# A two-block gated transformer kernel on one core: one clip pass in five moved to another engine, first key transfers shared, the entry of the second attention reordered

## The reference, cut to what matters

```python
# block 1: cross attention, 16 heads of 16, with projections, softmax replaced by
s = where(scores >= 0, scores + 1, 1 / (1 - scores)); attn = s / sum(s)
# block 2: mixture of 64 experts, top 8, capacity 128, and a shared expert of 512
# block 3: attention of layernorm(x) on the raw context, plain softmax
out = softmax(q k^T) v
# block 4: 256 -> 1024, butterfly of 10 stages, gelu, butterfly, 1024 -> 256
```

## Time and profile before

| | |
|---|---|
| median of 3 runs | 1233.26 us (1229.75 to 1236.8) |
| the profiled execution | 1231.84 us |
| its span in the profile | 1229.6 us |
| PE busy | 1034.0 us, 84% |
| VectorE (DVE) busy | 817.2 us, 66% |
| ScalarE (ACT) busy | 702.2 us, 57% |
| GpSimd (POOL) busy | 360.6 us, 29% |
| mean granted TensorE clock | 0.927 of full speed |

### The profile page before, as it was taken

How to read it: one execution, slowest core, us unless ns; L and a number is a source line. 1 busy time by engine, 2 the same in 40 slices (tenths; PEclk the granted TensorE clock), 3 DMA queues, 4 the chain that set the end, 5 groups by cost and what they waited for, 6 DMA issues and landing times.

```text
span 1229.6 us, 17473 instructions
## 1 busy us (share of the span) xinstructions
PE 1034.0 (84%) x5635; PEld 751.7 (61%) x5635; DVE 817.2 (66%) x2051; ACT 702.2 (57%) x1351; POOL 360.6 (29%) x313
## 2 busy tenths in 40 slices
PE   4688888888876688998899976888898989899888
PEld 2354544544444577887687755657676767767567
DVE  4468778777778766755667658687567577664543
ACT  1899878988975433565554421364455455544542
POOL 2000000000000003778777631124334251423223
PEclk9779988988887888999999996899999999999998
DMA  6564435434121323788988644331312133120000
GB/s 145 122 153 137 129 95 167 120 82 129 52 73 69 128 61 104 184 203 199 245 198 184 146 119 92 88 109 26 106 46 80 37 104 82 50 56 1 20 18 18
DMA packets 97401, 128.41 MB, mean 104 GB/s; under 512 B 26976, under 2 KB 69344, under 8 KB 97056
## 3 DMA queue, kind: packets, MB, share of 16 engines
q1 hardware_dynamic: 82448, 105.73, 30.0%
q0 software_dynamic: 12288, 18.88, 8.5%
q10 hardware_dynamic: 2576, 2.69, 1.0%
HBM read 66.15 MB, written 30.70 MB: 79 GB/s over the span
## 4 chain that ended last, share of the span: by engine, by line
PE 51%; DVE 26%; ACT 9%; issue 6%; POOL 3%; DMA 2%; SPq 2%; ACTq 2%; DVEq 0%; POOLq 0%
PE psum L912 6%; PE psum L1098 6%; PE psum L1083 5%; PE psum L1001 4%; PE psum L928 4%; PE psum L819 3%; DVE stats L1363 3%; PE psum L795 3%; PE psum L865 3%; PE psum L1030 2%; DVE weights L1484 2%; DVE peaks L1764 2%; PE psum L960 2%; PE psum L741 2%; DVE normed L1404 2%
## 5 line engine op out<-in xcount | busy, mean ns | idle before, releaser
L1863 POOL TENSOR_SCALAR vareps<-moments 128x4 f32<-128x4 f32 x32 | 10.4, 326 | 529.2 <-DVE moments L1366 529.2
L795 PE MATMUL psum<-q_stack,k_stack 96*128 96x512 f32 (+1 forms) x256 | 123.2, 511 | 39.2 <-DVE weights L1484 24.8
L1297 ACT ACTIVATE weights<-psum 128x512 f32<-128x512 f32 x160 | 94.1, 597 | 71.7 <-PE psum L795 60.7
L1484 DVE SCALAR_TENSOR_TENSOR weights<-psum,weights 128x512 f32<-128x512 f32 x160 | 102.5, 681 | 43.2 <-ACT weights L1162 43.0
L1883 POOL DMA_INDIRECT expert_sums<-made,sum_rows x64 | 105.4, 1647 | 59.3 <-DVE made L1734 38.6
L1910 POOL TENSOR_TENSOR hidden<-hidden_whole,hidden 128x512 fp32r<-128x512 f32 x64 | 82.3, 1287 | 114.2 <-DVE hidden L1812 114.2
L1030 PE MATMUL psum<-k_stack,q_stack 96*128 96x256 f32 x256 | 88.2, 395 | 31.9 <-DVE peaks L1764 20.0
L1764 DVE TENSOR_REDUCE peaks<-psum 128x2 f32<-128x308 f32 x256 | 107.0, 469 | 12.1 <-PE psum L1032 11.6
L912 PE MATMUL psum<-feat_parts,w_shared_up 128*128 128x512 f32 x384 | 100.5, 412 | 10.7 <-DVE shared_silu L1608 6.3
L1098 PE MATMUL psum<-w_con_high,hidden 128*128 128x256 f32 x512 | 102.2, 298 | 0.1
L1812 DVE CAST hidden<-hidden_whole 128x512 fp32r<-128x512 f32 x64 | 52.7, 823 | 71.6 <-ACT hidden_whole L1326 70.3
(11 more groups left out here) (211 smaller groups left out, 2390.9 us busy)
## 6 DMA issues: line engine op xcount, KB each, us to landing
expert_w<-in_expert_w SPq DMA_DIRECT2D x64, 384.0 KB
q_stack<-q_stage SPq DMA_DIRECT2D x96, 128.0 KB, 3.0
q_stack<-q_stage SPq DMA_DIRECT2D x174, 64.0 KB, 2.0
expert_sums<-zeros SPq DMA_DIRECT2D x6, 1408.0 KB, 8.2
fetched<-expert_sums SPq DMA_DIRECT2D x16, 512.0 KB, 4.8
rows_scratch<-rows SPq DMA_DIRECT2D x8, 640.0 KB, 3.4
k_raw<-in_k SPq DMA_DIRECT2D x16, 300.0 KB
x<-in_x SPq DMA_DIRECT2D x8, 512.0 KB, 4.8
```

Source lines behind the costliest of these rows:

```text
L795: T.matmul(to, k[0:row, head_at(head), :], q[0:row, head // 2, :], start=True, stop=True).then_inc(scored, 1)
L1297: A.activation(weights1[n % 6][:, :], score_bank[n % 2], ACT.Exp).then_inc(exped, 1)
L1484: V.scalar_tensor_tensor(weights[n % 9][:, :], score_bank[n % 5], 1.0, weights[n % 9][:, :], ALU.add, ALU.max).then_inc(weighted, 1)
```

## The change

It does these things:

- First attention: the clip of each group's fifth chunk (32 of 160) is done by VectorE (`clip_last`) and listed one round earlier, behind the weights of the group's first pair; the log of that chunk waits for it on a semaphore of its own. An empty step is put between `turn_att` and `att_feats`.
- Start: of batch 0's 12 key DMAs ScalarE issues 6 (places 0 and 1); SP issues its queries of places 0 and 1, then queries and keys of places 2 and 3. GpSimd's clearing waits for the first norm. Two load semaphores are merged.
- Into the second attention: SP issues the loads of half 0's sums (in four DMAs, by pairs of tiles) and of the first two quarters of keys ahead of the barrier, once all sums have been written. VectorE adds by pairs of tiles and takes the statistics of each pair behind it. GpSimd's adds for half 1 wait for the four key residuals instead of the norm of half 0.
- Half 1: statistics and norm stand behind the maxima of half 0, the turned queries behind them, and all four sends are SP's. `PEAKS_SECOND` places the 16 maxima of half 1 at c = 1 to 11.

```diff
@@ after_steps
-    return [turn[0:2], divide[0:2] + turn[2:4], divide[2:4], [("turn_att", h)], [("att_feats", h)],
+    return [turn[0:2], divide[0:2] + turn[2:4], divide[2:4], [("turn_att", h)], [], [("att_feats", h)],
@@ plan_first
             plan += [("weight", n) for n in sets[i - 1]]
+        if i + 1 < len(sets) and len(sets[i + 1]) == 1:
+            plan.append(("clip_last", sets[i + 1][0]))
...
-        plan += [("clip", n) for n in now]
+        if len(now) > 1:
+            plan += [("clip", n) for n in now]
@@
-PEAKS_SECOND = (-1, -1, -1, -1, 1, 2, 3, 4, 5, 6, 7, 7, 8, 8, 9, 9)
+PEAKS_SECOND = (1, 2, 2, 3, 4, 4, 5, 6, 6, 7, 8, 8, 9, 10, 10, 11)
@@ plan_last
-    plan = [("fetch", 0), ("load_k1", 0, 0), ("load_k1", 0, 1)]
+    plan = []
...
-    beside_peaks = {4: norm_units("q1", 1)[:2], 7: norm_units("q1", 1)[2:],
-                    9: [("turn_q1", 1), ("send_q1", 1, 0), ("send_q1_a", 1, 1)]}
     for n in range(HT * PAIRS // 2):
         plan.append(("peak", 0, n % HT, n // HT))
-        plan += beside_peaks.pop(n, [])
         if n in LATE_AT:
             late.step()
-    plan.append(("peaks", 0))
-    plan += [("send_q1", 1, two) for two in range(2, PAIRS // 2)]
+    plan += [("peaks", 0)] + norm_units("q1", 1)
     late.step()
-    plan += peak_units(1, -1)
+    plan += [("turn_q1", 1)] + [("send_q1", 1, two) for two in range(PAIRS // 2)]
+    late.step()
     plan.append(("scores1", 0))
@@ ScalarE
                 if b == 0:
                     A.wait_ge(keys_split, 1)
-                    to_key_stack(A, 0)
+                    to_key_stack(A, 0, (0, 1))
...
             def log(n):
-                A.wait_ge(clipped, n + 1)
+                if n % 5 == 4:
+                    A.wait_ge(clipped_last, n // 5 + 1)
+                else:
+                    A.wait_ge(clipped, n // 5 * 4 + n % 5 + 1)
@@ VectorE
+            def clip_last(n):
+                if n >= 9:
+                    V.wait_ge(weighed, weighed_by(n - 9))
+                V.wait_ge(scored, n + 1)
+                V.tensor_scalar(weights[n % 9][:, :], score_bank[n % 5], -1.0, 0.0, ALU.mult,
+                                ALU.max).then_inc(clipped_last, 1)
...
-            def add_experts(h, i):
+            def add_experts(h, a):
                 if h == 0:
-                    V.wait_ge(fetched_in[i], 16)
-                    if i:
-                        V.wait_ge(x_first, i)
-                    V.tensor_tensor(half_of(0), half_of(0), fetched[i][:, :, :], ALU.add).then_inc(x_first, 1)
+                    tiles = slice(2 * a, 2 * a + 2)
+                    for i in range(SUMS):
+                        V.wait_ge(first_sums[SUMS * a + i], 32)
+                        if i:
+                            V.wait_ge(x_first, SUMS * a + i)
+                        V.tensor_tensor(x[:, tiles, :], x[:, tiles, :], fetched[i][:, tiles, :],
+                                        ALU.add).then_inc(x_first, 1)
+                    V.wait_ge(x_first, SUMS * (a + 1))
+                    for t in range(2 * a, 2 * a + 2):
+                        tile_stats(norm_no["q1", 0], 0, t)
@@ GpSimd
                     elif h == 1:
-                        G.wait_ge(ln_normed, HT * (norm_no["q1", 0] + 1))
+                        G.wait_ge(keys_split, BATCH + 4)
...
             def clear_rest():
+                G.wait_ge(ln_normed, HT)
@@ SyncE
-                send(S, q_stage, q_stack[h % 2][:, :, :], q_in[h % 2])
+                together = (0, 1) if h == 0 else range(4)
+                send(S, q_stage, q_stack[h % 2][:, :, :], q_in[h % 2], places=together)
+                if h == 0:
+                    S.wait_ge(keys_split, 1)
+                    for r in (2, 3):
+                        send(S, q_stage, q_stack[0][:, :, :], q_in[0], places=(r,))
+                        to_key_stack(S, 0, (r,))
...
+            def fetch_first():
+                for i in range(SUMS):
+                    S.wait_ge(scattered[i], 16 * (EXPERTS // SUMS))
+                for a in range(2):
+                    for i in range(SUMS):
+                        S.dma_start(fetched[i][:, 2 * a:2 * a + 2, :], sum_dram[i][2 * P * a:2 * P * (a + 1), :].rearrange(
+                            "(t p) f -> p t f", p=P)).then_inc(first_sums[SUMS * a + i], 16)
...
                     S.drain().then_inc(stage_over, 1)
+                    if n == 2:
+                        fetch_first()
+                        load_k1(0, 0)
+                        load_k1(0, 1)
                     S.wait_ge(stage_over, 5 * n)
```

37 lines of the change are left out of this document (20 added, 17 removed).

## The result

The changed kernel takes 1261.19 us in the median of 4 runs (1259.42 to 1264.49), the kernel before 1233.36 beside it (4 runs): a ratio of 1.0237, with a 95% interval of 1.0204 to 1.0269. It is 28 us slower; the prediction said 26 us faster. The profiled execution took 1262.6 us, its span is 1260.5.

What follows compares the result with a forecast made beforehand. ScalarE was taken to bound the first attention, a chain across engines the passage into the second. Start −7, steady −15, tail +1 and passage −5 sum to −26: from the median of 1233.26 to 1207.3 us, range 1192 to 1228.

Steps and rivals of the forecast that it cites:

- ScalarE is the bound there: First attention's body, 35 to 355 us: ScalarE, at work 289.66 of 320 us, sets the pace.
- relief term: First attention, steady: 32 clips of 0.62 us leave ScalarE, 19.8 us less at most, taken as −20.
- Rival 3: First attention: no new waits, half of the old one goes; steady −27, in all −38, 1195 us; 12%.
- rival 1: First attention: VectorE's lag decides everywhere, steady part gives 0, start and passage stay; −11, 1222 us; 20%.
- Rival 4: First attention: VectorE becomes the bound, keeps its waits, its clips add 21.8 us; in all +11, 1244 us; 9%.
- steady part: First attention's loop: −20 clips, −6 empty step, +11 new waits, so −15 us; bounds −35 and +21.8.
- (a) to (d): Passage: early sums and moved GpSimd adds −2.9 us, half 1's norm work leaving half 0's maxima −5.4, its return net 0.
- (d): Passage: half 1's norm and turned queries return behind half 0's maxima, about 11 us instead of 8 before first scores; net 0.
- (b): Passage: GpSimd's adds for half 1 no longer slow a shared expert's residual (2.768 us, usually 0.692); some 0.6 us won.
- (e): Second attention's loop: four of half 1's maxima, hidden in a wait before, join it; 3.4 us.
- (f): Passage: SP sends half 1's 24 query pieces before fetching half 2's sums; up to 4 us of VectorE's wait.
- Rival 2: Passage gives nothing, since its loop stalls for half 2's sums; in all −21, 1212 us; 16%.

Runs made afterwards that it cites:

- b3: a3 without the fifth chunks' clip (log reads scores with scale 0, output differs), so ScalarE has 32 passes less, VectorE none more: 1230.95 us, ratio 0.9986.
- b2: a3 with 32 VectorE passes over constants in the place of its clips, for which nobody waits: 1241.22 us, ratio 1.0098.
- a1: The changed kernel without the empty step, fifth chunks' clips still on VectorE: 1248.44 us, ratio 1.0115.
- d3: b4 with an empty step behind the norm, so all behind the norm comes one step later: 1242.36 us, ratio 1.0087.
- c4: b4 with only the 16 maxima of half 1 at the changed kernel's places in the loop: 1232.36 us, ratio 0.9988.
- a3: The changed kernel without the empty step and with all 160 clips on ScalarE: 1231.40 us, ratio 0.9976.
- a4: The changed kernel with half 2's sums and two key quarters issued ahead of half 1's last two pairs of query sends: 1261.96 us, ratio 1.0227.
- b4: a3 with half 1's norm, turned queries, sends and maxima placed as in the kernel before: 1222.73 us, ratio 0.9925.
- d2: b4 with the additions to x alone one step later: 1220.32 us, ratio 0.9914.
- d4: b4 with the norm's statistics one step earlier, in one step with the additions: 1222.57 us, ratio 0.9917.
- d1: b4 with the norm's statistics alone one step later, directly ahead of the norm: 1237.29 us, ratio 1.0044.
- e1: d1 with four PE products, results overwritten, ahead of PE's wait for the normed rows: 1230.65 us, ratio 0.9968.

## Why the prediction was wrong

**The step that failed first is "ScalarE is the bound there".** It was read from busy shares, 289.66 of 320 us. b3 is the test: 32 passes gone and nothing added is worth 4.1 us in the traced execution and nothing in the medians, not 19.8. The relief term of −20 was at least about five times too large. My reading, which no run tests by itself: per group of heads every engine waits for another in turn (scores, exponentials, weights, bank), and a pass off one link returns only where that link ends a wait. Rival 3 fell with it. ScalarE's idle time was also not "mostly one wait": the 15.0 us are half of its 30.3.

**VectorE's load** was sized about rightly, by the pass (0.684 against 0.68) and by the price: I took +11 for the new waits, and b2 measures 11.2 for the 32 passes alone (15.0 by the ratios), with 1 to 2 more for the log's wait. But I had set it against 20. The clips then come out at +8.6 by themselves (17.1) where −9 stood; rival 1 (VectorE's lag takes the relief) named the mechanism and stopped at 0. Rival 4 had the sign and half of the mechanism: VectorE's clips do go on the path, but at 11.2 us and not at their full 21.8, and it is not the bound (busy 253.13 of 320 us in a1, 237.03 in the changed kernel). Rival 4's bound for the steady part, +21.8, was passed too, since neither it nor the forecast gave the empty step a loss.

**The empty step** is the term with the largest error. I had counted it as −6 (bounds 0 and −15), for the wait for the attention rows, and never asked what it does to the fifteen steps behind it. That wait did go, and as large a one stands before the gate's rows. The step as put costs 18.8 alone and 22.8 on top of the clips (392.7 to 415.5). d3 shows that moving all behind the norm is enough for that (23.3 us). What the traces show there is gate and shift in one round, with VectorE waiting 17.1 us for the gate product (1.2 before); which of the units behind the norm costs the time (gate, shift, exponential, top, counts) was not tried apart. In sum the steady part is +29.6 in the loop (323.7 to 353.3) where −15 stood.

**Start.** −7 against −7.3: right, both terms within 0.6 us; clip at 28.0 (28.5 forecast), norm 1.39 us, ScalarE's six issues 6.01. The issues began 1.5 us earlier where the norm was to give 1.0. The price of an issue is the trace's: 1.00 us each while SP issues too, 0.64 for SP's 24 later ones. The rule of the Trainium skill (Trainium Kernel Development and Optimization, Key Constraints) is that issuing from several engines saves issue time only. Read as the prediction read it, six issues at a lone queue's price, ScalarE would have been free sooner than at 27.35. It was the keys' landing (first scores at 27.19) and then the scores that set the clip, so its time can't tell the two.

**Tail.** 59.4 to 64.5 us from the last exponential to the next stage over all kernels, 60.4 before and 62.2 after; +1 can't be told from 0.

**Passage.** Up to the first exponential the forecast holds: last write to there 62.7 and 57.6 us, −5.1 where (a) to (d) summed to −8.3; the second add waits no more, the maxima of half 0 take 15.9 instead of 20.1, but (d), "net 0", is +2.3 (9.1 to 11.4). (b) came out as forecast: GpSimd's adds lie behind the first norm's followers, and no residual of the shared expert takes over 0.724 us (2.768 before). The last residual, which the prediction's −3 would have had held by the moved adds, took 0.693 at 770.8; the adds had ended at 769.9, so this run doesn't test it. The failed term is the 3.7 for (e) and (f): halves 0 and 1 of the loop take 105.9 instead of 94.6 us, 11.3 lost. It is (e), the places of the maxima: c4 alone loses 9.6 us of median (7.8 by the ratios), more than the 7.4 that I had called the most for (e) and (f) together; (f) is there (3.10 us of wait, 4 at most forecast), a3 has the same plan without such a wait and a passage no shorter (165.2 us), and a4 removes its cause without a gain in the medians. I priced the four maxima that join the loop and not the other twelve, which all move to later places, up to c = 11. Which of the places does it was not tried. Rival 2 (the passage gives nothing) was nearer, and it too stopped at 0.

By parts, before rounding: −7.3 + 29.6 + 6.2 = +28.5; the medians differ by 27.8, the profiled executions by 30.8.

## What to carry to other kernels

A busy share of 90% doesn't make an engine the bound where each waits for the others in turn: before pricing a relief, take the work away and see what comes back (here a fifth at most). In a hand-written order, an empty step isn't a wait of one step; it moves every step behind it, and for each of these one has to ask whether it now shares a round with the step that feeds it. A profile of one execution prices a stage to a few us only; compare it with the ratios of the medians before splitting a loss into parts. The best kernels found keep the start, the early loads, the pairwise statistics and GpSimd's later adds, and leave half 1 as it was: b4, d2 and d4 (the last two with additions or statistics one step off), at 0.9914 to 0.9925 of the time before.

## What the runs showed of the hardware that was not expected

Passes of VectorE for which nobody waits cost 0.35 us each (b2, 11.2 over 32; 0.47 by the ratios) of the 0.680 us that they last, though VectorE is idle a quarter of the loop. An issue of a small DMA took ScalarE 1.00 us while SP issued too, where SP alone took 0.64. And with most stands of PE of 1.9 to 4.4 us in one piece (30 of 35) the granted clock falls to its lower level: 67.7 us of the loop in b4 with one such stand a half, 98 to 108 with two (d1, d3). Products put into the stands brought the clock back (98.5 to 70.8 us in e1) and the traced loop hardly any time (336.5 to 335.7).
